# Splitting the negated score maxima on GpSimd instead of VectorE, and multiplying with the values before the maxima are turned

## What is computed

```python
attn = jnp.einsum('nhqd,nhkd->nhqk', q, k) * scale
attn = jnp.where(causal, attn, -jnp.inf)
attn = jax.nn.softmax(attn, axis=-1)
out = jnp.einsum('nhqk,nhkd->nhqd', attn, v)
```

## Time and profile before

| | |
|---|---|
| median of 3 runs | 696.56 us |
| the profiled execution | 694.38 us, span 692.7 us |
| TensorE matmul | 569.9 us (82% of the span), 4419 instructions |
| VectorE | 476.6 us (69%), 1171 |
| ScalarE | 337.0 us (49%), 646 |
| GpSimd | 222.5 us (32%), 224 |
| chain that ended last | TensorE 36%, VectorE 18%, GpSimd 4%, issue 3%, ScalarE 3% |

### The profile page before, as it was taken

How to read it: one execution, slowest core, us unless ns; L and a number is a source line. 1 busy time by engine, 2 the same in 40 slices (tenths; PEclk the granted TensorE clock), 3 DMA queues, 4 the chain that set the end, 5 groups by cost and what they waited for, 6 DMA issues and landing times.

```text
span 692.7 us, 12790 instructions
## 1 busy us (share of the span) xinstructions
PE 569.9 (82%) x4419; PEld 386.9 (56%) x4470; DVE 476.6 (69%) x1171; ACT 337.0 (49%) x646; POOL 222.5 (32%) x224
## 2 busy tenths in 40 slices
PE   3586999899887869889986898588979999986565
PEld 1443566665544338778965665345646565454444
DVE  4689677759875525765556657767867877647993
ACT  2022667667666724435533241436656676763221
POOL 6411010222234322460554025422030103254664
PEclk9999999999999989999999899889999999999885
DMA  8527796856321131222324004203012100000001
GB/s 257 138 75 158 169 240 146 177 122 128 65 61 44 42 101 32 62 75 57 89 54 111 27 17 128 56 22 95 25 37 85 49 25 27 27 0 1 15 17 30
DMA packets 51294, 53.43 MB, mean 77 GB/s; under 512 B 6975, under 2 KB 44081, under 8 KB 51201
## 3 DMA queue, kind: packets, MB, share of 16 engines
q1 hardware_dynamic: 49185, 48.42, 27.5%
q0 software_dynamic: 2048, 4.20, 2.2%
HBM read 33.56 MB, written 21.10 MB: 79 GB/s over the span
## 4 chain that ended last, share of the span: by engine, by line
PE 36%; DVE 18%; POOL 4%; issue 3%; ACT 3%; DMA 1%; SPq 1%; POOLq 0%; DVEq 0%; ACTq 0%
PE ps L630 5%; PE ps L1245 5%; DVE mx L826 4%; PE ps L611 4%; PE ps L587 4%; PE ps L1233 2%; PE ps L656 2%; PE ps L590 2%; ACT pT L713 1%; PE ps L614 1%; PE ps L1224 1%; DVE xn L1139 1%; PE ps L1226 1%; PE ps L1227 1%; PE ps L1225 1%
## 5 line engine op out<-in xcount | busy, mean ns | idle before, releaser
L826 DVE TENSOR_REDUCE mx<-ps 128x2 f32<-128x1024 f32 (+2 forms) x192 | 196.0, 1040 | 64.3 <-PE ps L590 63.1
L713 ACT ACTIVATE pT<-ps 128x512 f32<-128x512 f32 x320 | 182.8, 596 | 54.0 <-PE ps L614 50.7
L590 PE MATMUL ps<-mask_qk,identb 128*128 128x128 bf16 (+2 forms) x352 | 87.1, 248 | 3.6 <-DMA stB<-max_scratch 1.1
L614 PE MATMUL ps<-mask_kq,identb 128*128 128x128 bf16 (+1 forms) x320 | 81.3, 254 | 4.4 <-issue 2.6
L630 PE MATMUL ps<-pT,vA 128*32 128x512 f32 (+3 forms) x1024 | 77.0, 435 | 1.4 <-ACT pT L713 1.4
L611 PE MATMUL ps<-stB,kA 128*128 128x384 bf16 (+3 forms) x241 | 56.2, 302 | 11.6 <-ACT pT L713 11.1
L587 PE MATMUL ps<-kA,stA 128*128 128x384 bf16 (+3 forms) x245 | 54.6, 304 | 8.7 <-DVE mx L826 8.4
L587 PE MATMUL ps<-stA 128*128 128x384 bf16 (+3 forms) x247 | 55.1, 303 | 6.9 <-DVE mx L826 3.7
L611 PE MATMUL ps<-stB 128*128 128x384 bf16 (+3 forms) x240 | 55.6, 299 | 5.6 <-ACT pT L713 4.4
L630 PEld LDWEIGHTS ps<-pT,vA 128*32 128x32 f32 x1024 | 39.9, 110 | 31.4 <-issue 20.7
L1269 ACT ACTIVATE pT<-ps 128x512 f32<-128x512 f32 x46 | 27.4, 596 | 61.2 <-PE ps L1227 61.1
(11 more groups left out here) (296 smaller groups left out, 1114.5 us busy)
## 6 DMA issues: line engine op xcount, KB each, us to landing
stA<-stack_scratch SPq DMA_DIRECT2D x48, 192.0 KB, 3.3
stB<-stack_scratch SPq DMA_DIRECT2D x48, 192.0 KB, 4.0
stack_scratch<-part SPq DMA_DIRECT2D x12, 384.0 KB, 3.1
stack_scratch<-part SPq DMA_DIRECT2D x12, 256.0 KB, 3.1
pairs_scratch<-b1r SPq DMA_DIRECT2D x46, 64.0 KB
pT<-pairs_scratch SPq DMA_DIRECT2D x46, 64.0 KB, 1.9
outs_scratch<-pT SPq DMA_DIRECT2D x46, 64.0 KB
w_lo<-w_scratch SPq DMA_DIRECT2D x8, 256.0 KB, 4.0
```

The costliest lines, as they stand in the source:

```text
L590: last = pe.matmul(diagonal, identb[:], mask_qk[:].unsqueeze(1).broadcast_to([P, per, P]), start=False, stop=True)
L614: last = pe.matmul(blocks, identb[:], mask_kq[:].unsqueeze(1).broadcast_to(blocks.shape), start=False, stop=True)
L713: act.activation(dst_, src, ACT.Exp, scale=SCALE).then_inc(a["ex"], 1)
L826: nc.vector.tensor_reduce(mx[:, g % 2, qb, heads[0]:heads[0] + nh], src, AX.X, ALU.max).then_inc(a["maxd"], 1)
```

## The change

MP moves from VectorE's to GpSimd's part of the list, at the same place of the order. It has five instructions there instead of four: subtraction from zero to a float32 tile of its own (`mneg`), copy to the high part, subtraction, copy to the middle part, subtraction. The waits are the same. In all four groups PV now stands ahead of MT, for TensorE, ScalarE and GpSimd alike.

```diff
--- before.py
+++ after.py
@@ -113,12 +113,12 @@
                 late = [turned[0], keys, turned[1]]
             early = [[], [], tokens, queries] if behind else [tokens, queries, turned[0]]
             misc = {
-                0: [[("MP", s - 1, 3)], [("MT", s - 1, 3), ("PV", s - 2, 3), ("VA", s - 1, 0)], early[0],
+                0: [[("MP", s - 1, 3)], [("PV", s - 2, 3), ("MT", s - 1, 3), ("VA", s - 1, 0)], early[0],
                     [("OT", s - 2, 3)], *early[-2:]],
-                1: [[("MP", s, 0)], [("MT", s, 0), ("PV", s - 1, 0)], *late, [("OT", s - 1, 0), ("KM", s + 1, 0)]],
-                2: [[("MP", s, 1)], [("MT", s, 1), ("PV", s - 1, 1), ("SPLITQ", s + 1, 0), ("SPLITK", s + 1, 0)], [("WO", s - 2, 0)] * layer, [("LN", s + 2, 0)],
+                1: [[("MP", s, 0)], [("PV", s - 1, 0), ("MT", s, 0)], *late, [("OT", s - 1, 0), ("KM", s + 1, 0)]],
+                2: [[("MP", s, 1)], [("PV", s - 1, 1), ("MT", s, 1), ("SPLITQ", s + 1, 0), ("SPLITK", s + 1, 0)], [("WO", s - 2, 0)] * layer, [("LN", s + 2, 0)],
                     [("OT", s - 1, 1)], []],
-                3: [[("MP", s, 2)], [("MT", s, 2), ("PV", s - 1, 2)], [("V", s + 1, 0)], [("NORM", s + 2, 0)],
+                3: [[("MP", s, 2)], [("PV", s - 1, 2), ("MT", s, 2)], [("V", s + 1, 0)], [("NORM", s + 2, 0)],
                     [("OT", s - 1, 2)], []],
             }[g]
             def scores(*units):
@@ -372,6 +372,7 @@
         stB = sb("stB", [KR, 2, 2 * HG, T], BF16)
         fill = sb("fill", [3, T], BF16)
         mx = sb("mx", [P, 2, NB, HG])
+        mneg = sb("mneg", [P, NB, HG])
         mrest = sb("mrest", [P, NB, HG])
         mpart = sb("mpart", [P, 2, NB, 3, HG], BF16)
         mrow = sb("mrow", [32 + 3 * HG, T], BF16)
@@ -824,17 +825,6 @@
                 else:
                     src = ps[:, pair, :].rearrange("p (h k) -> p h k", k=w)
                 nc.vector.tensor_reduce(mx[:, g % 2, qb, heads[0]:heads[0] + nh], src, AX.X, ALU.max).then_inc(a["maxd"], 1)
-            elif name == "MP":
-
-                dve.wait_ge(a["maxd"], (i + 1) * NS)
-                if i >= 2:
-                    dve.wait_ge(a["mt"], i - 1)
-                m = mx[:, g % 2]
-                hi, mid, lo = (mpart[:, g % 2, :, k, :] for k in range(3))
-                link(nc.vector, nc.vector.tensor_tensor(hi, fixed[:, 2:3].unsqueeze(2).broadcast_to(m.shape), m, ALU.subtract))
-                link(nc.vector, nc.vector.scalar_tensor_tensor(mrest[:], m, -1.0, hi, ALU.mult, ALU.subtract))
-                link(nc.vector, nc.vector.tensor_tensor(mid, mrest[:], mrest[:], ALU.max))
-                nc.vector.tensor_tensor(lo, mrest[:], mid, ALU.subtract).then_inc(a["mpart"], 1)
             elif name in ("LN", "NORM"):
                 norm_vector(dve, 2 * B * layer + b, name, b, (ld_x[b], 16) if layer == 0 else (M["acc"], (b + 1) * NB))
             elif name == "OT":
@@ -861,6 +851,18 @@
             i = b * G + g
             if name == "LN":
                 norm_gpsimd(pool, 2 * B * layer + b)
+            elif name == "MP":
+
+                pool.wait_ge(a["maxd"], (i + 1) * NS)
+                if i >= 2:
+                    pool.wait_ge(a["mt"], i - 1)
+                m = mx[:, g % 2]
+                hi, mid, lo = (mpart[:, g % 2, :, k, :] for k in range(3))
+                link(nc.gpsimd, nc.gpsimd.tensor_tensor(mneg[:], fixed[:, 2:3].unsqueeze(2).broadcast_to(m.shape), m, ALU.subtract))
+                link(nc.gpsimd, nc.gpsimd.tensor_copy(hi, mneg[:]))
+                link(nc.gpsimd, nc.gpsimd.tensor_tensor(mrest[:], mneg[:], hi, ALU.subtract))
+                link(nc.gpsimd, nc.gpsimd.tensor_copy(mid, mrest[:]))
+                nc.gpsimd.tensor_tensor(lo, mrest[:], mid, ALU.subtract).then_inc(a["mpart"], 1)
             elif name in ("QM", "KM") and layer == 0:
                 c = "QK".index(name[0])
                 pool.wait_ge(a[name[0].lower() + "mid"], b + 1)
```

## The result

The changed kernel takes 710.2 us (median of four runs, 705.47 to 713.26); beside it the kernel before took 696.39. The ratio is 1.019, interval 1.015 to 1.023: slower, by some 13.5 us where 7.2 had been forecast. The profiled execution has a span of 707.8 us, 15.1 more than the 692.7 of before.

What follows compares the result with a forecast made beforehand. VectorE was taken to bound the first sequence's scoring and partly the routing stretch, TensorE the steady groups. Terms -3.2 - 4.0 + 2.2 + 5.8 + 6.4 = +7.2 us on the median 696.56 gave 703.8 us, range 695.0 to 710.0.

Steps and rivals of the forecast that it cites:

- Start of layer 0: First four splits, in a VectorE-bound stretch, leave VectorE: -3.2 us, ends -0.8 and -3.4.
- Filled waits: TensorE's other waits for the split, five groups, filled by the product with the values: -4.0 us, ends -3.2 and -4.7.
- Length of the split: GpSimd's five operations with links take 1.5 us, about 290 ns each of three; the product hides it on TensorE.
- Gathers: Start of layer 1: splits (0,2) and (0,3) queue behind GpSimd's gathers; +5.8 us, low end 4.6, high end 8.
- Split (2,1): Layer 0, sequence 2: split queues behind GpSimd work, TensorE waits 2.8 us against 0.54; net +2.2, ends +0.8 and +2.5.
- Exchange of product and turning: 24 groups: later maxima copy delays exponential and shared bank's next user; +6.4 us, floor 0, ceiling 9.6.
- The loads behind the later copy: SyncE waits about 3 us longer for the copy, transfers queue behind; costed at nothing, 3 us once without cover.
- The step that failed: Start of layer 1: the new 5.4 us wait may bring another low-clock stretch; counted inside the high end of 8.
- Bank hidden: Rival: ScalarE's and the bank's delay in the exchange is absorbed; 697.4 us, chance 0.17.
- Faster by VectorE: Rival: VectorE sets the pace in more steady groups, 0.84 us counting in 24; 690.8 us, chance 0.15.
- GpSimd slow: Rival: 1.1 us an operation, split 5.5 us, beyond the cover in 24 steady groups; 757 us, chance 0.03.
- Gathers taken up: Rival: the wait behind the gathers at layer 1's start is taken up later; 698.0 us, chance 0.13.

Runs made afterwards that it cites:

- run nine: The kernel before with only the four splits of the first sequence of layer 0 on GpSimd, old order; 694.70 us, ratio 0.9975.
- run eleven: The changed kernel with the operations of GpSimd's split made twice; 728.75 us.
- run four: The changed kernel with splits (0,2) and (0,3) of layer 1 and (2,1) of layer 0 back on VectorE; 700.73 us.
- run three: The changed kernel with only splits (0,2) and (0,3) of layer 1 back on VectorE; 704.52 us.
- run one: The kernel before with only the order changed, product ahead of turning in all four groups, split still on VectorE; 707.83 us, ratio 1.016.
- run five: The kernel before, in which only ScalarE copies the product's output ahead of the turned maxima; 712.48 us, ratio 1.025.
- run eight: The kernel with the order alone changed, but the old order again in sequence 2, group 3 of layer 0; 702.41 us against 707.83.
- run seven: The changed kernel with 24 matmuls without use ahead of the turning (0,2) of layer 1; 708.62 us.
- runs six: The changed kernel with the turning moved to a later place, behind LN in the third group, at the end of the others; 700.79 us, ratio 1.009.

## Why the prediction was right and where it was not

**Direction and places: right. Size: half.** Slower was given 0.68, and slower it is. But +7.2 us were forecast and 13.3 to 13.8 came (ratio, medians). The ratio puts the kernel at 709.9 us, just inside the range (710.0), the median of 710.2 just outside. That it comes out so near is luck in part: the range was made from the ends of other terms, and these came out near their middles; what filled it is a clock cost of which it held one small piece, elsewhere.

**Start of layer 0**, -3.2 forecast: -2.8 in the profile; alone it stays -2.0 (run nine).

**Filled waits**, -4.0: -3.2 by the steps of the three large ones (0.79, 1.31 and 1.96 us, all gone), which also hold the exchange of these groups. That VectorE's load takes some of it back isn't shown.

**Length of the split**, 1.5 us: 1.4. GpSimd's two-operand operation of 128x16 measured 217 to 229 ns against the 290 worked out, and 0.9 to 1.3 times VectorE's means. The Trainium skill (GPSIMD Engine Reference, section Engine selection) has about twice; at 16 columns the trace doesn't agree. By the 2.0 ns a column of the earlier trace rows, an estimate, 16 columns are only 32 ns of GpSimd's 217 to 229. In the groups with cover the choice of engine costs nothing that the profile shows (run eleven); in the three late splits it does, 9.5 us by the medians of the changed kernel and run four.

**Gathers**, +5.8: +5.5 in the profile between the two layers. The medians of run three give 5.0 to 5.7, and its profile 5.8: from the turning (0,1) to the first product of layer 1 the changed kernel loses 6.05 us, run three 0.22. The turning waited 5.11 us (5.4 forecast), the next one came 8.2 us later than (0,1)'s shift would have it (13.36 - 5.17; 8.9 forecast).

**Split (2,1)**, +2.2: the wait was 2.75 us as forecast (2.8), with the 0.54 of before off +2.2. The step was +3.5, of which 0.6 is the exchange (the same step in runs one and four). That leaves 2.9, so the granted clock behind it (0.89 and 0.92 in the windows 132 to 140 and 140 to 150 us, 1.00 before and in run four) cost at most 0.15 us.

**Exchange of product and turning**, +6.4: its mechanism is shown by run five, with both branches (the exponential's, the bank's). Its own size was near: 0.3 to 0.6 us in a group that shows it, +4.0 in layer 1 and, in layer 0, +1.3 in the first five steady groups with 0.77 us of filled waits taken off. But run one gave +12 instead of 6.4 less the filled waits. In its profile 4.2 us of that are the eighth product's step (run eight), 2.5 the thirteenth's, beside a low clock again, and 2.9 come in the expert stage, where nothing was changed; why is open.

**The loads behind the later copy**, put at nothing: TensorE waits 3.9 us for loads of `stA` and `stB`, before 4.2. Right.

**The step that failed** is the sentence of the prediction that such a wait also costs clock, with the cost placed behind the gathers and put "inside the high end". There filling the wait gained about 1 us (run seven). It costs most where I had not looked: the step of 4.2 us behind a 0.68 us wait for the bank at 152 us (run eight: 5.4 us by the medians). It very likely also makes most of the 2.7 us at the end of layer 0. There the expert router's first small matmul now waits 1.21 us for the bank, where in the kernel before it didn't wait, and from 216 to 220 us the clock is low:

```profile
213.28 0.36 PE L1188 MATMUL ps<-cpT,q 128*128 128x8 f32 x2 [1.21 <-ACT mrow L721]
...
216.00:220.00 4.00, 3.67 (x17) 1.94 (x17) 1.29 (x7) 2.88 (x6) 1.75 (x2) 0.59 0.02 4
```

The thirteenth product's step is +2.3 us here, and +2.5 to +2.7 in runs one, five and eight, each with a wait of 1.2 to 1.4 us at that place and a low clock behind it; in runs six and nine the clock there is 1.00 and the step at most 0.1. No run changed that wait alone, so this part is argued. The sum by the profile: +7.2, 0.4 for the start, 0.8 for the filled waits, -0.3 for the gathers, 0.2 for split and exchange together (8.8 measured, 8.6 forecast), and 4.2 and 2.7 for the two steps that had not been foreseen, are 15.2, as measured. So 6.9 of the 8.0 us that the forecast lacked are these two steps.

**The rivals.** Bank hidden: refuted by runs one and five. Faster by VectorE: refuted; 22.5 us of VectorE's work went and paid 2.8 us at the start (the 3.2 of the filled waits are the order's: run one has 2.9 of them with the split on VectorE). GpSimd slow: refuted by the durations. Gathers taken up: refuted by run three.

## What to carry to other kernels

Ask of every step that is moved where its consumer's copy lands: a 0.6 us copy in a gap is free, the same copy behind the event that ends the gap delays all that waits for it, here some 0.3 to 0.6 us in a group, and 12 us in 24 groups with what it costs in clock. Work given to an engine that is idle on average waits behind whatever its in-order list puts ahead; look up the few places (gathers, here) before the average. Move only the pieces whose engine is the bound or whose wait the profile names: four of 32 splits moved were 2.1 us ahead in the profile (the medians can't tell), seven of them, with the order changed in three groups, gained 3, and all 32 lost 14.

## What had not been expected of the hardware

One added wait of TensorE of 0.69 us, 2 us ahead of small matmuls of the expert router (128x8 and 128x1), went in run one with a granted clock of 0.66 from 156 to 166 us (0.69 in the changed kernel); without it the same work ran at 1.00 (run eight), and with 0.39 us in its place too (run five). In the low stretch TensorE runs at the lower of two levels: four transposes that take 0.61 us in all at full clock took 1.06 at 160 us of the changed kernel. So an added wait of 0.7 us cost 4.2, six times itself, and one of 0.4 us cost nothing beyond itself.

VectorE's norm of four 128x128 pieces took 2.36 us where GpSimd ran one operation after another, against 1.12 to 1.14 in ten other places of the profile. The Trainium skill (GPSIMD Engine Reference, section Key points) says that the two share their SBUF interfaces, with contention when VectorE has two SBUF inputs, as it has here (`x` and `rstd`); the row agrees:

```profile
133.08 1.17 POOL L869 TENSOR_TENSOR part<-q,part 128x512 bf16<-128x512 f32 x1
133.83 2.36 DVE L1141 SCALAR_TENSOR_TENSOR w_sb<-x,mv,rstd 128x128 f32<-128x128 f32 x4
...
134.20 1.32 POOL L1093 TENSOR_TENSOR w_lo<-w_lo,w_hi 128x512 fp32r<-128x512 f32 x1
```

The split itself met this in the kernel before: an operation of 128x16 that usually takes 0.17 us took 1.03 while GpSimd had one of 512 columns, and 1.20 and 1.13 at 180.83 and 503.74 us. These few lift the means of the earlier trace rows from 0.17 to 0.21 and 0.23 us.

```profile
87.55 1.16 POOL L867 TENSOR_TENSOR part<-q,part 128x512 bf16<-128x512 f32 x1 [1.80 <-ACT part L744]
87.70 1.03 DVE L836 TENSOR_TENSOR mpart<-mrest 128x16 bf16<-128x16 f32 x1
```
